# Giving out the final scatters of a graph-network kernel without a wait for their descriptors

## The chip, the cores and the metric

The kernel runs on one core of a Trainium2 chip. The metric is the device time of one execution in microseconds (us), lower is better. Engines: TensorE (PE in the profile, PEld for its weight loads), VectorE (DVE), ScalarE (ACT), GpSimd (POOL) and SyncE (SP), each with its own instruction stream and synchronised by semaphores alone.

## What is computed

`x` has 100,000 rows of 128 float32 values; there are 25,000 edges `src -> dst`, sorted by `dst`. Two graph layers follow each other, each with a residual and a layer norm. Cut to what matters:

```python
dst = minimum(int(100000 * uniform(25000) ** 2.0), 99999)     # then sorted

def _L0_gnn_ref(x, edge_index, W1, b1, W2, b2):
    row, col = (edge_index[0], edge_index[1])
    x_col = x[col]
    feat = jnp.concatenate([x_col, x[row] - x_col], axis=-1)
    messages = jax.nn.relu(feat @ W1 + b1) @ W2 + b2
    out = jax.ops.segment_max(messages, col, num_segments=x.shape[0])
    return jnp.where(jnp.isneginf(out), jnp.zeros_like(out), out)

def _L1_gnn_ref(x, edge_index, W1, b1, W2, b2, Wres, bres):
    agg = jax.ops.segment_sum(x[src], dst, num_segments=x.shape[0])
    h = jnp.maximum((x + agg) @ W1 + b1, 0.0) @ W2 + b2
    return x @ Wres + bres + h

x = _layernorm(x + _L0_gnn_ref(x, ...))
x = _layernorm(x + _L1_gnn_ref(x, ...))
```

Most rows are the `dst` of no edge. For them both sums are zero, and the result is a dense function of the row alone.

## The kernel before, in words

**Two kinds of work.** The dense work computes every one of the 100,000 rows as though it had no edge, and stores it to `out`. The edge work computes the rows that have edges and writes them over the dense result by scatters. `dst` is cut into groups of 512 edges (`ROWS`), 49 of them (`GROUPS`), each of four tiles of 128 (`TILES`): 196 tiles. The dense rows are cut into 196 units of 512 rows; four units are a body of 2,048 rows, and there are 49 bodies.

**Stages.** `walk` (line 310) lays out the same order on every engine: one dense body; the search for places of `src` among the edges (`step_s`); the edge pass of the first layer (`step_a`); that of the second (`step_b`); and dense bodies alone to the end. Dense units are woven into all of them. The second edge pass ends by writing its rows into the large SBUF buffer `edge_rows` (`finish1`, lines 1214 to 1222), which counts `res_done` up once per group.

**Dense units.** SP loads 512 rows into `x_in` (`load`, line 370), DVE normalises them (`norm1_scale`, line 712, whose multiplication is the helper's line 682), PE transposes and multiplies, ACT writes `o_rows` (line 1123) and SP stores them (line 385), counting `stored[k]` up by 16 per unit, k being the unit's place in its body.

**POOL.** Apart from some constants it only issues indirect DMAs: 196 gathers of `x` rows by `src`, 196 by `dst`, 196 of the table of first-layer results, and behind them the 196 scatters of `edge_rows` to `out`. All are issued one after the other in straight-line code. The scatter loop (lines 638 to 656) does this for each group:
- it waits until the scatters of four groups ago have landed (`final[r]`) and until the second edge pass has written the group (`res_done`);
- it waits until the dense stores have passed the group: the count comes from `stores_16`, in which DVE has put, from the group's last `dst`, 16 times the number of the body that holds it; `stores_needed` (line 634) loads it ahead of the last tile of the group before. The last, incomplete group (line 648) waits for all 49 bodies;
- it issues four scatters of 128 rows. Rows that are not the last edge of their `dst` have an index out of bounds and are dropped.

Line 656 waits for the landing of all scatters.

Of the kernel before, what the change touches and what calls it, by code (L numbers as in the profile page):

```python
# [44 lines left out]
def gnn_program(nc, x, src, dst, e_w1, e_b1, e_w2, e_b2, w1, b1, w2, b2, wres, bres, out):  # L45
    N, D = x.shape
# [20 lines left out]
    with ctx:  # L67
# [487 lines left out]
        def _(pool):  # L555
# [16 lines left out]
            def pace(kw):  # L572

                issued[0] += 1
                if issued[0] % 2 == 0:
                    kw["engine_sem"] = s_issued

            def issued_pair():
                if issued[0] % 2 == 0:
                    pool.wait_ge(s_issued, issued[0] // 2)  # L580
# [7 lines left out]
                issued_pair()  # L588

            def scatter(table, frm, t, done):  # L590
                kw = {}
                pace(kw)
                nc.gpsimd.indirect_dma_start(table, bass.IndirectOffsetOnAxis(idx[:, SCAT, t:t + 1], 0), frm, None,  # L593
                                             bounds_check=N - 1, oob_is_err=False, **kw).then_inc(done, 16)
                issued_pair()

            def gather_src(g):
                j, r = divmod(g, SLOTS)
# [41 lines left out]
            for g in range(GROUPS):  # L640
                j, r = divmod(g, SLOTS)
                wait(pool, final[r], 16 * TILES * j)
                pool.wait_ge(res_done, g + 1)
                if g < WHOLE:
                    for k in range(SLOTS):
                        pool.wait_ge(stored[k], count)
                    pool.nop().then_inc(s_turn, 1)
                elif g == WHOLE:
                    for k in range(SLOTS):
                        pool.wait_ge(stored[k], 16 * BODIES)  # L650
                for t in range(TILES):
                    if t == TILES - 1 and g + 1 < WHOLE:
                        count = stores_needed(g + 1)
                    scatter(out, edge_rows[:, cut(g * TILES + t)], g * TILES + t, final[r])
# [817 lines left out]
```

## Time and profile before

| | us |
|---|---|
| median of 3 runs | 1343.35 |
| lowest and highest run | 1338.25, 1344.81 |
| profiled execution | 1332.02 |
| its span, from first to last instruction | 1330.2 |
| mean granted TensorE clock | 0.952 |

| engine | busy us | share of the span |
|---|---|---|
| PE | 1123.7 | 84% |
| DVE | 1068.6 | 80% |
| POOL | 825.8 | 62% |
| ACT | 799.8 | 60% |

How to read it: the shares are means over all stages, and the stages have different limits, so the stretches and the end of the run have to be looked at one by one. POOL's busy time is the time in which it works at indirect DMAs, not the time in which data moves. "issue" as a releaser means that the profile shows nothing that the engine waited for. A line marked q (POOLq, SPq) is the engine's sequencer.

### The profile page before, as it was taken

To read this page: it belongs to the slowest core of one execution; us is meant where nothing else is said; L and a number is where in the kernel's file an instruction comes from. 1 tells how busy PE (TensorE), PEld (TensorE's weight loads), DVE (VectorE), ACT (ScalarE), POOL (GpSimd) and SP (SyncE) were. 2 spreads that over 40 slices of the span, in tenths; PEclk is the share of its full clock that TensorE was granted. 3 is DMA by queue.
4 is the path that set the end of the run, shared out by engine and by line. 5 is a ranking of instruction groups with operands and counts; after the bars stand their busy time and mean duration, and the time that the engine had idled before them with its cause. 6 is when DMAs were issued, how large, how long until landed. Compare 5 with 4: busy or idle time off the path is not lost. (4 is left out here: it accounts for less than half of the span.)

```text
span 1330.2 us, 32137 instructions
## 1 busy us (share of the span) xinstructions
PE 1123.7 (84%) x7512; PEld 853.2 (64%) x7512; DVE 1068.6 (80%) x5491; ACT 799.8 (60%) x2305; POOL 825.8 (62%) x797
## 2 busy tenths in 40 slices
PE   2699999998888878788759999999999999999500
PEld 1577777765555545455448888888887777777400
DVE  6599999989887887898838999999987888888400
ACT  0366666666665656667526666666666777777400
POOL 5666666656666666666256666666665666655654
PEclk9899999999998999999979999999999999999855
DMA  4477777756665667666436565656564556656310
GB/s 111 141 220 214 214 220 212 222 188 195 183 208 180 199 174 210 177 205 196 141 112 191 187 185 186 185 187 187 189 190 140 177 181 190 185 181 200 103 38 28
DMA packets 160366, 233.86 MB, mean 176 GB/s; under 512 B 26815, under 2 KB 69273, under 8 KB 160284
## 3 DMA queue, kind: packets, MB, share of 16 engines
q1 hardware_dynamic: 133612, 193.69, 46.7%
q0 software_dynamic: 25088, 38.81, 11.0%
q10 hardware_dynamic: 1584, 0.53, 0.2%
q14 instruction: 62, 0.51, 0.1%
q8 instruction: 20, 0.33, 0.1%
HBM read 129.48 MB, written 90.12 MB: 165 GB/s over the span
## 5 line engine op out<-in xcount | busy, mean ns | idle before, releaser
L1277 PE MATMUL psY<-wcr,xT 128*128 128x128 f32 x1568 | 305.0, 276 | 0.0
L1276 PE MATMUL psY<-wc,hT 128*128 128x128 f32 x1568 | 304.6, 276 | 0.0
L586 POOL DMA_INDIRECT edge_rows<-x1e_table,idx x196 | 210.8, 1075 | 133.2 <-DMA edge_rows<-x1e_table,idx 77.6
L593 POOL DMA_INDIRECT out<-edge_rows,idx x196 | 202.2, 1031 | 129.5 <-issue 76.4
L586 POOL DMA_INDIRECT edge_rows<-in_x,idx x196 | 206.9, 1056 | 116.0 <-DMA edge_rows<-in_x,idx 67.3
L586 POOL DMA_INDIRECT xd_rows<-in_x,idx x196 | 203.5, 1038 | 115.9 <-DMA xd_rows<-in_x,idx 67.3
L1276 PEld LDWEIGHTS psY<-wc,hT 128*128 128x128 f32 x1568 | 255.8, 193 | 15.0 <-issue 8.3
L1123 ACT ACTIVATE o_rows<-psY,rs_b 128x128 f32<-128x128 f32 x784 | 223.0, 367 | 66.7 <-DVE rs_b L741 66.5
L1277 PEld LDWEIGHTS psY<-wcr,xT 128*128 128x128 f32 x1568 | 239.9, 193 | 0.0
L1287 PE MATMUL psH<-xT,wc 128*128 128x512 f32 x392 | 204.5, 604 | 16.0 <-DVE deltas L787 10.6
L1103 ACT ACTIVATE sd_a<-mv_a,eps_col 128x4 f32<-128x4 f32 x196 | 58.3, 298 | 239.6 <-DVE mv_a L677 239.6
L672 DVE BATCH_NORM_STATS2 bn_b<-psY 128x6 f32<-128x128 f32 x784 | 174.4, 285 | 21.9 <-PE psY L1277 7.9
L691 DVE BATCH_NORM_STATS2 bn_a<-x_in 128x6 f32<-128x128 f32 x784 | 173.1, 271 | 0.3 <-DMA x_in<-in_x 0.3
L1267 PEld LDWEIGHTS psT<-ident,x 128*128 128x128 f32 x784 | 99.5, 143 | 106.2 <-issue 104.9
L1092 ACT ACTIVATE hT<-psH,bias_cols 128x512 f32<-128x512 f32 x196 | 131.0, 669 | 5.0 <-PE psH L1287 5.0
L682 DVE TENSOR_TENSOR x<-x_in,rs_a 128x512 f32<-128x512 f32 x196 | 130.6, 666 | 0.3 <-PE psT L1267 0.3
L1267 PE MATMUL psT<-ident,x 128*128 128x128 f32 x784 | 119.5, 276 | 0.9 <-DVE idx L1055 0.9
L1267 PE MATMUL psE<-ident,xs_rows 128*128 128x128 f32 x392 | 61.8, 281 | 60.8 <-ACT ehT L1161 51.6
L1100 ACT COPY xT<-psT 128x512 f32<-128x512 f32 x196 | 112.5, 574 | 0.5 <-PE psT L1267 0.5
L1267 PEld LDWEIGHTS psE<-ident,xs_rows 128*128 128x128 f32 x392 | 45.9, 143 | 98.2 <-issue 83.0
L923 DVE TENSOR_TENSOR_SCAN shared<-mask,shared,psE 128x512 f32<-128x512 bf16 x48 | 61.4, 1279 | 36.5 <-PE psE L1267 23.5
L1287 PEld LDWEIGHTS psH<-xT,wc 128*128 128x128 f32 x392 | 65.8, 194 | 35.6 <-issue 11.0
(135 smaller groups left out, 2042.6 us busy)
## 6 DMA issues: line engine op xcount, KB each, us to landing
x_in<-in_x SPq DMA_DIRECT2D x196, 256.0 KB
out<-o_rows SPq DMA_DIRECT2D x196, 256.0 KB
xs_rows<-edge_rows SPq DMA_DIRECT2D x98, 256.0 KB, 2.9
xs_rows<-src_dram SPq DMA_DIRECT2D x49, 256.0 KB, 4.3
mask<-mask_dram SPq DMA_DIRECT2D x98, 128.0 KB, 3.6
x1e_table<-shared SPq DMA_DIRECT2D x49, 256.0 KB, 2.8
x1eT_spill<-x1eT SPq DMA_DIRECT2D x49, 256.0 KB
x1eT<-x1eT_spill SPq DMA_DIRECT2D x49, 256.0 KB, 2.8
```

The source lines that it names most:

```text
L586: nc.gpsimd.indirect_dma_start(to, None, table, bass.IndirectOffsetOnAxis(idx[:, what, t:t + 1], 0), bounds_check=rows - 1, oob_is_err=err ...
L593: nc.gpsimd.indirect_dma_start(table, bass.IndirectOffsetOnAxis(idx[:, SCAT, t:t + 1], 0), frm, None, bounds_check=N - 1, oob_is_err=False ...
L672: last = v.bn_stats(bn[:, t, :], rows[:, cut(t)])
L682: v.tensor_tensor(tiles(to), tiles(rows), rs.unsqueeze(2).broadcast_to([P, TILES, P]), ALU.mult).then_inc(done, 1)
L691: last = v.bn_stats(bn_a[:, k % 2, t, :], x_in[:, k, cut(t)])
L1092: a.activation(hT[:, k % 2, :], psH[:, :], ACT.Relu, bias=bias_cols[:, 2:3]).then_inc(hT_done, 1)
L1100: a.copy(xT[:, k, :], psT[:, :]).then_inc(xT_done, 1)
L1123: last = a.activation(o_rows[:, k, cut(t)], psY[k % 2][:, cut(t)], ACT.Copy, scale=rs_b[:, k, t:t + 1])
L1267: last = t_.transpose(to[:, cut(t)], rows[:, cut(t)], ident[:, :])
L1276: t_.matmul(to[:, cut(t)], h[:, cut(t)], wc2[:, :], start=False, stop=False, skip_group_check=True)
L1277: last = t_.matmul(to[:, cut(t)], xt[:, cut(t)], wcr[:, :], start=False, stop=t == TILES - 1, skip_group_check=True)
L1287: t_.matmul(psH[:, :], wc1[:, :], xT[:, k, :], start=True, stop=True).then_inc(w1_done, 1)
```

## The change

The helper that issues the scatters no longer calls `pace` and `issued_pair`. The scatters carry no semaphore for their descriptors and no wait stands behind them. The gathers still count and wait by pairs; 588 of them come before the first scatter, an even number. The waits for landings, for `res_done` and for the dense stores are all kept.

```diff
             def scatter(table, frm, t, done):
-                kw = {}
-                pace(kw)
                 nc.gpsimd.indirect_dma_start(table, bass.IndirectOffsetOnAxis(idx[:, SCAT, t:t + 1], 0), frm, None,
-                                             bounds_check=N - 1, oob_is_err=False, **kw).then_inc(done, 16)
-                issued_pair()
+                                             bounds_check=N - 1, oob_is_err=False).then_inc(done, 16)
```

## Rows read from the trace of the kernel before

**Rows 1.** Busy time of each engine in four stretches of the end; DMA queues

```profile
core 0: us, PE busy (x) PEld busy (x) DVE busy (x) ACT busy (x) POOL busy (x), PEclk, DMA share, GB/s
...
1060.00:1130.00 70.00, 69.62 (x470) 54.71 (x469) 61.80 (x389) 54.40 (x164) 44.12 (x42) 1.00 0.61 187
1130.00:1200.00 70.00, 69.61 (x474) 54.94 (x473) 61.61 (x388) 54.92 (x164) 43.27 (x40) 1.00 0.61 183
1200.00:1256.00 56.00, 49.27 (x338) 39.35 (x336) 40.89 (x254) 40.53 (x123) 33.44 (x34) 0.98 0.52 164
1256.00:1331.00 75.00, 0.00 (x0) 0.00 (x0) 0.00 (x0) 0.00 (x0) 39.88 (x41) 0.50 0.11 33
...
q0 software_dynamic: 25088, 38.81, 11.0%
```

**Rows 2.** The end: last scatters, waits of SP and POOL, DRAIN (count: ns, starts)

```profile
1318.73 0.98 POOL L593 DMA_INDIRECT out<-edge_rows,idx  x1 [0.81 <-DMA out<-edge_rows,idx]
1320.02 0.98 POOL L593 DMA_INDIRECT out<-edge_rows,idx  x1 [0.30 <-issue]
...
L656 POOLq EVENT_SEMAPHORE  x2: 43/1508/2974, 1319.1 to 1319.2; - x2
...
L67 POOLq DRAIN  x1: 7589/7589/7589, 1322.4 to 1322.4; - x1
...
L550 SPq EVENT_SEMAPHORE  x2: 17/22/27, 1253.7 to 1255.0; - x2
```

**Rows 3.** POOL's timeline: first pair of scatters, and two groups behind the dense loop

```profile
991.37 1.02 POOL L593 DMA_INDIRECT out<-edge_rows,idx  x1 [2.00 <-issue]
992.69 1.00 POOL L593 DMA_INDIRECT out<-edge_rows,idx  x1 [0.30 <-issue]
...
1303.06 0.98 POOL L593 DMA_INDIRECT out<-edge_rows,idx  x1 [1.08 <-issue]
1304.35 0.98 POOL L593 DMA_INDIRECT out<-edge_rows,idx  x1 [0.30 <-issue]
1306.14 0.98 POOL L593 DMA_INDIRECT out<-edge_rows,idx  x1 [0.81 <-DMA out<-edge_rows,idx]
1307.43 0.98 POOL L593 DMA_INDIRECT out<-edge_rows,idx  x1 [0.30 <-issue]
1309.49 0.98 POOL L593 DMA_INDIRECT out<-edge_rows,idx  x1 [1.08 <-issue]
```

**Rows 4.** All 196 scatters: durations, first and last start, what POOL waited for

```profile
L593 POOL DMA_INDIRECT out<-edge_rows,idx x196: 975/982/1417, 991.4 to 1320.0; - x196
its engine sat idle before it (us, times) until:
  issue: 76.4, 134
  DMA out<-edge_rows,idx: 40.8, 50
  DMA out<-o_rows: 11.5, 10
```

**Rows 5.** Scatters as a group, from 1016 to 1200 us and from 1256 us on

```profile
L593 POOL DMA_INDIRECT out<-edge_rows,idx x107 | 114.1, 1066 | 70.9 <-issue 40.3 <-DMA out<-edge_rows,idx 21.3 <-DMA out<-o_rows 9.3
...
L593 POOL DMA_INDIRECT out<-edge_rows,idx x41 | 40.2, 981 | 25.4 <-issue 16.5 <-DMA out<-edge_rows,idx 9.0
```

**Rows 6.** POOL's sequencer: loading the count, and its last waits on stores

```profile
L635 POOLq TENSOR_LOAD <-stores x48: 284/290/809, 989.4 to 1305.9; - x48
L635 POOLq FUSED_REGOPS  x48: 147/147/181, 990.0 to 1306.2; - x48
...
L646 POOLq EVENT_SEMAPHORE  x2: 43/43/43, 1302.1 to 1308.5; - x2
```

**Rows 7.** SP's timeline around three dense stores (units 183, 191 and 195)

```profile
1216.62 0.42 SPq L385 DMA_DIRECT2D out<-o_rows  x1
...
1241.45 0.33 SPq L385 DMA_DIRECT2D out<-o_rows  x1
...
1252.94 0.33 SPq L385 DMA_DIRECT2D out<-o_rows  x1
```

**Rows 8.** Timeline where a scatter begins beside the multiplication of line 682

```profile
1067.80 0.69 DVE L682 TENSOR_TENSOR x<-x_in,rs_a 128x512 f32<-128x512 f32 x1
...
1067.94 1.40 POOL L593 DMA_INDIRECT out<-edge_rows,idx  x1 [0.81 <-DMA out<-edge_rows,idx]
```

**Rows 9.** All runs of line 682 from 1016 to 1200 us

```profile
L682 DVE TENSOR_TENSOR x<-x_in,rs_a x54: 655/658/692, 1016.3 to 1198.4; 128x512 f32<-128x512 f32 x54
```

## The prediction, made before the changed kernel was built or run

> **What bounds the kernel now.** I read the engines by stretch first, then the end of the run, then POOL's waits, then single scatters in order of time.
>
> By stretch [rows 1], PE is busy for 69.6 of 70 us up to 1200 us, so the dense loop sets the time there, with DVE second at 61.6 to 61.8. After 1256 us PE, DVE and ACT do nothing, and POOL alone works on: 41 scatters. This is the whole case: the dense loop stores its last rows and the span goes on for some 74 us in which only the scatters of line 593 are left.
>
> The end [rows 2]: the last stores have landed at 1255.0 us (SP's wait on line 550), the last scatter begins at 1320.02, POOL's wait for landings began at 1319.17 and took 2.97 us, and a DRAIN of 7.59 us follows. From the last scatter's start to the end of the span (1330.2) it is 10.2 us. The chain of waits names only that last scatter, so it doesn't tell why it was so late; the timeline does.
>
> The spacing [rows 3, 4]: 196 scatters start between 991.4 and 1320.0, one per (1320.0 - 991.4) / 195 = 1.685 us. In a quiet group, behind 1256 us, one takes 0.98 us. Between the two of a pair the engine is idle for 0.30 us; behind a pair it is idle 0.81 us inside a group and 1.08 us between groups, where POOL's sequencer also goes through the waits on the stores. So a pause costs 0.51 or 0.78 us over the bare spacing, and POOL's own waits [rows 4] tell the same: 76.4 us of "issue" and 40.8 us behind scatters, but only 11.5 us for the dense stores. POOL is hardly ever held by the data it scatters over; it is late because of its own rate.
>
> **What the change does, step by step.** It removes line 594's semaphore and line 595's wait. Nothing is added, no transfer is added or taken away, and the 588 gathers ahead of 991 us are as before, so I take the first scatter to start at 991.4 still.
>
> *The spacing without pauses.* Inside a pair it is 0.98 + 0.30 = 1.285 us (1303.06 to 1304.35, [rows 3]). No row shows a third scatter behind a second without a pause, so this has to be bounded. From below: 1.285, since the second of a pair had nothing to wait for and still came 0.30 us behind the first. From above: the present mean, 1.685. I go by the second of a pair, the nearest row, because only the number in the queue differs. Where the dense loop runs beside them the scatters are longer: the mean is 1.066 us from 1016 to 1200 us and 0.981 behind 1256 [rows 5], so I use 1.066 + 0.305 = 1.371 for the whole stretch with dense work.
>
> *Does the sequencer keep up?* Per group it has to load the count (0.29 us, with 0.15 us of register work) and go through the waits. But its wait of line 656 starts at 1319.1 us, before the last scatter starts on the engine at 1320.02 [rows 2], and the load at the fourth scatter of a group leaves the gap at 0.30 us as often as not [rows 3, 6]. It runs at least one instruction ahead, so I cost both at nothing; their cover is the 0.98 us of the scatter that is running. Were the cover gone, it would be the 0.27 us by which 1.08 exceeds 0.81, times 48 groups: 13 us.
>
> *POOL's clock.* The last group is the 49th: 192 scatters lie ahead of it. They take 192 x 1.371 = 263.2 us, so POOL comes to it at 1254.6 us; by the bare 1.285 it would be 1238.1.
>
> *The dense stores.* A group may go once all bodies up to the one that holds its last row are stored. By the way in which dst is drawn, the last row of group g lies near 100000 x (512 (g + 1) / 25000)^2. For g = 46 that is 92,700, body 45, whose last unit (183) is stored from 1216.62 us on; for g = 47 it is 96,600, body 47, unit 191, issued at 1241.45 us [rows 7]. I add the 2.1 us from 1252.94 to 1255.0 for landing: 1218.7 and 1243.6. POOL reaches these groups at 991.4 + 184 x 1.371 = 1243.7 and 991.4 + 188 x 1.371 = 1249.1, later than both. The 49th needs every store: 1255.0. That is what is late next. The two meet almost exactly (1254.6 against 1255.0), and any faster spacing gains nothing more.
>
> *The end.* From the last wait on the stores to the scatter behind it takes 1.0 us (1308.5 to 1309.49, [rows 6, 3]): first scatter of the last group at 1256.0, fourth at 1256.0 + 3 x 1.285 = 1259.9, end of span 10.2 us later at 1270.1. The span falls by 60.1 us.
>
> *What the faster scatters do to the dense loop.* The same bytes are moved in about four fifths of the time. The DMA engines are at 0.61 of their time there [rows 1] and all software transfers are 11% of the whole run's, so I expect some 0.03 more, and no cost. DVE: the scale of line 682 and the scatters meet. Where a scatter starts inside line 682's run it takes 1.40 us in place of 0.98 (start at 1067.94 beside a scale from 1067.80 to 1068.49, [rows 8]); where the scale starts inside a scatter it stays at 655 to 692 ns over all 54 of them [rows 9]. So the waiting is all on POOL's side, it is in the 1.066, and DVE loses nothing.
>
> The Trainium skill speaks against this (SBUF — State Buffer, Who interferes with whom): a VectorE instruction with two inputs in SBUF and a GpSimd instruction that reads SBUF exclude each other, and whichever was issued first holds the other up to its end. The trace agrees for the scatter that comes second and not for the scale that comes second: no scale of the 54 is longer than 0.692 us. By the rule in full a scale would often wait for a scatter, which is rival D.
>
> *Against the runs shown.* The profiled execution took 1332.02 us beside its span of 1330.2, and is 11 us below the median of 1343.35. I take the difference in time, 60 us, off the median: 1283 us, 4.5% faster.
>
> **Rivals.**
>
> A, the spacing is longer than a pair shows. For: the durations vary with what runs beside them, and a queue with more in it may be slower. Against: the second of a pair is no longer than the first. At 1.45 us the last scatter starts at 991.4 + 195 x 1.45 = 1274.2, and the time is 14 us above the forecast, 1297; at 1.5 us 1307. Chance 0.12, some of it above 1305.
>
> B, the pause isn't what sets the rate: without it a third scatter waits as long for something else, for instance for an earlier one to leave the queue. A scatter lands about 2.1 us after its start [rows 2], so with two allowed in the air the spacing would be near 1.1, which speaks against it, but no row excludes another limit near 1.6. Then nothing changes: 1343. Chance 0.09. That the change doesn't do what it says is in this too: the wait on s_issued would be gone and the spacing stay.
>
> C, slower: scatters given out without a pause get longer themselves. It decides where busy time and gap exceed 1.72 us ((1320.0 + 6.7 - 991.4) / 195), that is with a scatter above 1.41 us. The longest of all 196 is 1.417 [rows 4], next to line 682. Were all as long as that, and the gaps no shorter than today's mean of (0.30 + 0.81) / 2 = 0.56 us, (1.417 + 0.56) x 195 = 386 us would put the end at 1387, 57 us up: 1400. Against: the mean of 1.066 leaves room for one such scatter in five, (1.066 - 0.981) / (1.40 - 0.98). Chance 0.05.
>
> D, the scale waits for scatters (the rule above). A scatter would be at work for 0.98 / 1.285 = 76% of the time in place of 0.98 / 1.6 = 61%; half its length is 0.49 us, so each of the 75 units would wait 0.07 us longer: 5 us if all of it reached PE. DVE is idle for 8 of 70 us [rows 1], which hides it. Time 1283 to 1288. Chance 0.02.
>
> **How the numbers follow.** My forecast has 0.72: spacing at most 1.39, the stores decide, 1283, own range 1275 to 1292. A has 0.12, B 0.09, C 0.05, D 0.02. A measurement of this kernel can tell about 0.5% from no change. Faster by more than that: forecast, D and A, 0.86. Same: 0.09. Slower: 0.05. The range runs from 1273 (a run as much below the forecast as the shown ones spread) to 1305, the larger part of A; B, C and the rest of A are left out, under 0.2.
>
> **What would show it.** Right: scatters 1.29 to 1.4 us apart with gaps of 0.30 us throughout; the wait behind POOL's last group named as the dense stores, from about 1250 to 1256 us; last scatter near 1260; span near 1270; PE's 69.6 of 70 us unchanged; scales still under 0.7 us. Wrong: gaps above 0.30 between scatters that wait for no store (B), durations above 1.1 us behind the dense loop's end (C), PE under 69 of 70 us (the faster scatters cost the dense loop), or a last store later than 1255.

## The result, and the profile after

The changed kernel took 1488.02 us, the median of 4 runs (1468.92 to 1489.70), beside 1340.80 us before (4 runs, 1337.31 to 1344.81): a ratio of 1.106, 95% interval 1.097 to 1.116. It is 10.6% slower; 1283 us was forecast. The profiled execution took 1488.20 us, its span is 1486.3.

A call (a series of runs on one chip, one after the other) came in one of two kinds; the versions that lose much in one kind lose nothing in the other, and the profile of before, on which the prediction rests, is of the other kind than the timed runs of after. The experiments tell how that was found.

First the scatters, answering to [rows 3, 4]. All of them, with what POOL waited for:

```profile
L591 POOL DMA_INDIRECT out<-edge_rows,idx x196: 979/982/1208, 999.2 to 1476.3; - x196
its engine sat idle before it (us, times) until:
  DMA out<-o_rows: 183.8, 10
  issue: 103.4, 186
```

POOL's timeline after the change: the first three, and the last two groups (start us, length us, engine, line, operation; in brackets the idle time before it and what ended it).

```profile
999.19 1.21 POOL L591 DMA_INDIRECT out<-edge_rows,idx  x1 [2.00 <-issue]
1000.70 1.00 POOL L591 DMA_INDIRECT out<-edge_rows,idx  x1 [0.30 <-issue]
1002.00 0.98 POOL L591 DMA_INDIRECT out<-edge_rows,idx  x1 [0.30 <-issue]
...
1464.28 0.98 POOL L591 DMA_INDIRECT out<-edge_rows,idx  x1 [0.30 <-issue]
1472.40 0.98 POOL L591 DMA_INDIRECT out<-edge_rows,idx  x1 [7.14 <-DMA out<-o_rows]
...
1476.26 0.98 POOL L591 DMA_INDIRECT out<-edge_rows,idx  x1 [0.30 <-issue]
```

The change did what it says. The gap is 0.30 us where POOL's own sequencer isn't held up with the others ("issue" is 0.56 us in the mean over 186 scatters, since some of it lies in the standstill told below), the wait for POOL's own completion is gone, no scatter is longer than before (1.208 us against 1.417 at most), and the waits behind which POOL stands are now those for the dense stores: 183.8 us in place of 11.5. POOL is no longer late by its own rate. It is the dense loop that is late, by stretch, to be held against [rows 1]:

```profile
core 0: us, PE busy (x) PEld busy (x) DVE busy (x) ACT busy (x) POOL busy (x), PEclk, DMA share, GB/s
1060.00:1130.00 70.00, 27.70 (x79) 18.46 (x79) 10.90 (x55) 7.43 (x21) 48.19 (x50) 0.54 0.22 69
1130.00:1200.00 70.00, 17.06 (x66) 11.68 (x65) 9.65 (x51) 8.60 (x27) 49.66 (x51) 0.56 0.19 60
1200.00:1256.00 56.00, 42.42 (x249) 32.91 (x250) 33.23 (x209) 30.07 (x89) 16.69 (x17) 0.82 0.37 115
1256.00:1331.00 75.00, 70.35 (x468) 54.77 (x468) 61.28 (x385) 54.53 (x165) 11.78 (x12) 1.00 0.48 151
```

In 70 us PE begins 79 matmuls where it began 470, the DMA engines move 69 GB/s in place of 187, and no engine but POOL is busy for more than 40% of the time. Everything but the scatters nearly stands still. The granted clock of 0.54 is a mean close to the lower level, 1.2 GHz. It fell between 1011 and 1012 us, and PE, still granted 1.00, had begun nothing from 1009 us on: the fall follows from the standstill. Nor do the transfers that are under way take longer: from 1060 to 1200 us the queue of the loads and stores moves 1,963 packets in 7.4% of the 16 DMA engines' time, 84 ns each, in place of 11,732 in 51.6%, 99 ns each. Fewer are given out. At 1221 us POOL has given out what it may (it waits for stores from there on), and the dense loop is back at its old speed. Seven dense stores are issued from 1012 to 1218 us, where it had been one every 3.4 to 11 us.

What it looks like inside shows in PE's timeline; these are matmuls of one accumulation (first of psY, then of psE), between which the code has no wait:

```profile
1060.98 0.37 PE L1273 MATMUL psY<-wc,hT 128*128 128x128 f32 x1 [0.83 <-issue]
1061.70 0.37 PE L1273 MATMUL psY<-wc,hT 128*128 128x128 f32 x1 [0.35 <-issue]
1062.42 0.57 PE L1274 MATMUL psY<-wcr,xT 128*128 128x128 f32 x1 [0.35 <-issue]
...
1084.60 0.37 PE L1273 MATMUL psE<-wc,ehT 128*128 128x128 f32 x1 [1.72 <-issue]
1087.41 0.37 PE L1274 MATMUL psE<-wcr,x1eT 128*128 128x128 f32 x1 [2.44 <-issue]
1089.51 0.37 PE L1274 MATMUL psE<-wcr,x1eT 128*128 128x128 f32 x1 [1.72 <-issue]
```

They start 0.72, 0.72, then 2.81 and 2.10 us apart: steps of about 0.70 us. "Issue" means that the profile shows nothing they waited for. I call a stretch of over 0.70 us in which none of PE, DVE, ACT and SP starts anything a silence. From the first scatter to the end of PE's work the trace of after has 83 of them, 127 us in all, most about 0.70 or 1.40 us long, the first at 1007 and the last at 1214 us. The trace of before has none. The silences are the plainest sign of the harm and not the whole of it: the last dense store, shown next, comes 216 us late.

The end answers to [rows 2, 7]. The last dense store, on SP:

```profile
1469.22 0.33 SPq L385 DMA_DIRECT2D out<-o_rows  x1
...
L67 POOLq DRAIN  x1: 7589/7589/7589, 1478.5 to 1478.5; - x1
```

It was 1252.94 us in the trace of before, which is of the other kind, so it is 216.3 us later. The prediction's working for the end, put behind this store, gives 1469.22 + 2.1 + 1.0 = 1472.3 for the last group (measured 1472.40), 1476.2 for the last scatter (1476.26) and 1486.4 for the span (1486.3). All that is wrong with the forecast is the time of the dense loop: 1270.1 + 216.3 = 1486.4.

### The profile page after: what moved, and what is told of

Read it like the earlier page. It is cut to its first block, busy times and chain, and to the rows that moved or that the text cites. A ratio compares the mean times of both kernels' runs of the same rounds, so it can differ in the third digit from the quotient of the medians.

```text
span 1486.3 us, 32134 instructions
## 1 busy us (share of the span) xinstructions
PE 1177.7 (79%) x7512; PEld 877.3 (59%) x7512; DVE 1071.3 (72%) x5491; ACT 802.0 (54%) x2305; POOL 809.5 (54%) x797
## 4 chain that ended last, share of the span: by engine, by line
PE 40%; DVE 22%; issue 15%; another core or an unknown queue 10%; ACT 7%; DMA 3%; SPq 1%; POOL 1%; DVEq 1%; ACTq 0%; POOLq 0%
PE psY L1274 7%; PE psY L1273 7%; PE psH L1284 6%; DVE bn_b L669 4%; PE psE L1264 4%; PE psT L1264 3%; DVE bn_a L688 3%; PE psY L1270 2%; PE psE L1274 2%; PE psE L1273 2%; DVE shared L873 2%; DVE x L679 2%; PE psE L1423 2%; ACT xT L1097 2%
## 5 line engine op out<-in xcount | busy, mean ns | idle before, releaser
L591 POOL DMA_INDIRECT out<-edge_rows,idx x196 | 192.8, 984 | 287.2 <-DMA out<-o_rows 183.8
L1273 PE MATMUL psY<-wc,hT 128*128 128x128 f32 x1568 | 310.1, 279 | 8.8 <-issue 8.8
L1274 PE MATMUL psY<-wcr,xT 128*128 128x128 f32 x1568 | 310.2, 279 | 6.9 <-issue 6.9
L586 POOL DMA_INDIRECT edge_rows<-x1e_table,idx x196 | 204.2, 1042 | 136.5 <-issue 99.9
L1273 PEld LDWEIGHTS psY<-wc,hT 128*128 128x128 f32 x1568 | 260.4, 196 | 26.2 <-issue 19.3
L1284 PE MATMUL psH<-xT,wc 128*128 128x512 f32 x392 | 211.2, 621 | 50.1 <-ACT xT L1097 38.9
L1274 PEld LDWEIGHTS psY<-wcr,xT 128*128 128x128 f32 x1568 | 244.0, 196 | 10.4 <-issue 10.4
L1264 PE MATMUL psT<-ident,x 128*128 128x128 f32 x784 | 122.7, 279 | 4.0 <-issue 3.1
L669 DVE BATCH_NORM_STATS2 bn_y<-psE 128x6 f32<-128x128 f32 x196 | 43.4, 284 | 97.6 <-remote 75.8
```

What stands on the lines that cost most here:

```text
L586: nc.gpsimd.indirect_dma_start(to, None, table, bass.IndirectOffsetOnAxis(idx[:, what, t:t + 1], 0), bounds_check=rows - 1, oob_is_err=err ...
L669: last = v.bn_stats(bn[:, t, :], rows[:, cut(t)])
L1264: last = t_.transpose(to[:, cut(t)], rows[:, cut(t)], ident[:, :])
L1273: t_.matmul(to[:, cut(t)], h[:, cut(t)], wc2[:, :], start=False, stop=False, skip_group_check=True)
L1274: last = t_.matmul(to[:, cut(t)], xt[:, cut(t)], wcr[:, :], start=False, stop=t == TILES - 1, skip_group_check=True)
L1284: t_.matmul(psH[:, :], wc1[:, :], xT[:, k, :], start=True, stop=True).then_inc(w1_done, 1)
```

## The experiments

Eighteen runs of fifteen kernels in six calls, each call on one chip. Where no interval is given a time is a single run. They are told in the order in which they ran, since what the first ten seemed to show fell with the later ones.

### Call 1 (chip 2; before 1346.87 us): how many scatters are handed over ahead, and how many go without a pause

Two kernels let POOL issue without a gap but only while at most 2 or 4 scatters are unfinished (`DEPTH`); two others put the old wait back behind every fourth or eighth scatter (`EVERY`).

```diff
+                if given[0] >= DEPTH:
+                    pool.wait_ge(s_given, given[0] - DEPTH + 1)
+                given[0] += 1
                 nc.gpsimd.indirect_dma_start(table, ...,
+                                             engine_sem=s_given).then_inc(done, 16)
```

```diff
+                given[0] += 1
+                if given[0] % EVERY == 0:
+                    kw["engine_sem"] = s_given
                 nc.gpsimd.indirect_dma_start(table, ..., **kw).then_inc(done, 16)
+                if given[0] % EVERY == 0:
+                    pool.wait_ge(s_given, given[0] // EVERY)
```

At most two unfinished. Expected:

> No pause, but the sequencer hands over a scatter only when at most one other is unfinished: one at work, one waiting. Spacing as in the changed kernel (gaps of 0.30 us). Theory Q (the queue of handed-over scatters, 5 to 7 deep when PE stopped in the changed kernel, is what starves the other engines): the dense loop keeps its pace, PE 69 of 70 us, last scatter near 1260, time 1275 to 1295. Theory W (what starves them is that POOL's engine works with gaps of only 0.30 us, whatever waits behind it): the dense loop stops as in the changed kernel, time above 1440.

At most four unfinished. Expected:

> The same with at most four unfinished. Theory Q: if the limit lies above four, the time of the run with two, 1275 to 1295; if it lies below, some stops, 1300 to 1488. Theory W: above 1440, the same as with two.

A pause behind every fourth. Expected:

> A wait behind every fourth scatter in place of every second. Mean spacing (0.98 x 4 + 0.30 x 3 + 1.08) / 4 = 1.48 us where no scale is in the way. Theory Q: at most three wait, so it should be as the run with four unfinished: last scatter near 1285, time 1295 to 1315. Theory W: gaps of 1.08 us every 6 us give the others some relief; between 1300 and 1440.

A pause behind every eighth. Expected:

> A wait behind every eighth scatter. Theory Q: up to seven can wait, as many as when PE stopped: clearly slower than before, above 1380, and PE's instructions missing in the last third of each eight. Theory W: above 1400.

Measured: 1471.76, 1487.93, 1388.03 and 1469.08 us. With at most two unfinished the loss is nearly whole (71 silences, scatters 1.287 us apart as in the changed kernel), where theory Q gave 1275 to 1295: the number that waits in POOL's queue is not the cause. A pause behind every fourth takes most of the lost time away (1388.03, in the range of theory W), but only about half of the dense loop's delay: its last store comes at 1368.9 us, 116 us behind the trace of before, and PE is busy for 50.57 and 56.30 of 70 us in the stretches from 1060 and from 1130 us, with 7 silences in all. So the loop also slows down without silences.

### Call 2 (chip 14; before 1333.46 us, 1332.20 to 1337.14, 7 runs): something else in the pause's place, threes, gathers, and a free tail

The first writes 128x512 int32 of zeros to a spare buffer behind every second scatter, with no wait; the second keeps the scatters in pairs and gives the gathers a wait behind every fourth; the third waits behind every third scatter (`EVERY = 3` above); the fourth keeps pairs up to scatter 160 and lets the last 36 run free.

```diff
+                if t % 2 == 1:
+                    wait(pool, s_fill, filled[0] - 3)
+                    nc.gpsimd.memset(filler[:, filled[0] % 4, :], 0).then_inc(s_fill, 1)
+                    filled[0] += 1
```

```diff
-                if issued[0] % 2 == 0:
-                    pool.wait_ge(s_issued, issued[0] // 2)
+                if issued[0] % 4 == 0:
+                    pool.wait_ge(s_issued, issued[0] // 4)
```

```diff
+                if t < FREE_FROM:
+                    pace(kw)
```

A write in place of the pause. Expected:

> No wait, but behind every second scatter POOL writes zeros over 128x512 int32 of a scratch buffer (one such took 0.52 us in the kernel before), so the scatters keep about the spacing of the pairs while POOL's engine gets no rest and its sequencer runs ahead by up to some seven scatters. Theory D (it is the scatters' own work, the writing of their descriptors, without a break of about 0.8 us in it): the dense loop keeps its pace, PE above 69 of 70 us, time near 1343. Theory W (any work of POOL's engine without rest): slow, above 1440. Theory Q (the queue), which the runs with two and four handed over speak against: slow as well.

Gathers by four, scatters in pairs. Expected:

> The kernel before with its 588 gathers waited for behind every fourth in place of every second; scatters in pairs. If what starves the engines comes with indirect DMAs of any kind (D or W), the stages before 990 us get longer, as the run with scatters by four did, by 5 to 40%: time above 1370, and the first scatter starts later than 1000 us. If it comes with scatters alone (their writes to HBM), the gathers end earlier or as before: time 1325 to 1345.

A pause behind every third. Expected:

> A wait behind every third scatter. Theories D and W: a burst of three lies between pairs (no loss) and fours (1388): the time is the sum of POOL's gain, 196 x 0.07 = 14 us, and what the dense loop loses; 1320 to 1365. If the loss sets in only at the fourth, 1330; if every burst of three costs as much as those of four, above 1370.

A free tail. Expected:

> The kernel before with pairs up to the 160th scatter and no wait from there on. In the trace of the kernel before the 160th comes at about 1259 us, when the dense loop has ended, so nothing is left to starve. Theories D, W and Q alike: 36 scatters at 1.285 in place of some 1.66 us: last scatter 13 us earlier, time 11 to 14 us less, near 1330. If the change itself costs something for another reason (a longer end), there is no gain.

Measured: 1302.78, 1320.64, 1311.36, and for the free tail 1324.27 us (1322.30 to 1324.82, 4 runs; ratio 0.992, interval 0.990 to 0.994). No silence in any. The write makes a gap of 0.72 us and a mean spacing of 1.53 us, and does no harm. Three of the four came out below every range that was given: the write was expected near the old spacing and 1343 us, the threes at 1320 or more, the gathers by four at 1325 or more; the free tail gained 9 us, where 11 to 14 were expected. So here it seemed that any rest for POOL will do, and that threes are harmless where fours are not. That comparison went across two calls, and it was a mistake.

### Call 3 (chip 5; before 1342.94 us): where the rest stands and how long it is

The same write in other sizes and places: two of 128x512 behind every fourth scatter, one of 128x256 behind each, one of 128x16 behind each; and the gathers without any wait, with the scatters in pairs.

```diff
+                if t % EVERY == EVERY - 1:
+                    for _ in range(REPS):
+                        wait(pool, s_fill, filled[0] - 7)
+                        nc.gpsimd.memset(filler[:, filled[0] % 8, :], 0).then_inc(s_fill, 1)
+                        filled[0] += 1
```

```diff
             def gather(to, table, what, t, done):
-                kw = {}
-                pace(kw)
...
-                issued_pair()
```

Fours with a rest. Expected:

> No wait; behind every fourth scatter two writes of 128x512 int32 (0.55 us each). Bare spacing (3 x 1.285 + 0.98 + 1.10 + 0.17) / 4 = 1.53 us on average, a little slower than the 1.49 of the run with one write behind every second, which cost the dense loop nothing. Theory B (what counts is how many scatters come in a row: three do no harm, four do): slow like the run with a wait behind every fourth, 1350 to 1400. Theory R (what counts is the mean rate: something takes up a scatter in about 1.5 us, and a backlog forms below that): as good as that run, 1300 to 1312.

A write behind each. Expected:

> No wait; behind every single scatter one write of 128x256 int32 (0.31 us): bare spacing 0.98 + 0.31 + 0.17 = 1.46 us, never two scatters in a row. Theory B: the dense loop untouched, last scatter near 1280, time 1285 to 1298. Theory R with a limit between 1.48 and 1.53: slow, 1350 to 1430.

A small write behind each. Expected:

> The same with a write of 128x16 int32, about 0.11 us: bare spacing about 1.26 us, no slower than the changed kernel's 1.285. Theory B, if any other instruction breaks the row: dense loop untouched, the stores decide, 1275 to 1285. Theory B, if it takes a break of some length, and theory R: 1440 to 1490.

Gathers without waits. Expected:

> The kernel before with no wait behind any of its 588 gathers; scatters in pairs. If the harm comes with any indirect DMA in long rows, the stages before 990 us get much longer: above 1450. If it comes with scatters alone, POOL's gathers end earlier: 1290 to 1325.

Measured: 1382.48 (5 silences), 1433.70 (17), 1487.07 (97) and 1774.31 us. Fours with writes stand where fours with waits stood (1388.03): it isn't the wait itself that heals. A rest behind each scatter, so that the short gap of 0.30 us is gone altogether, does worse (4 us above the range of theory R) than rests behind every fourth with gaps of 0.30 within: the short gap isn't what does the harm. Its mean spacing is shorter (1.48 against 1.53 us), which speaks for the rate; but these are single runs 3% apart in spacing, and where nothing else holds them up the fours with a wait come to 1.48 us as well (as expected above) and the write behind each to 1.473. That the rate decides is the simplest reading, not shown; that a long rest helps more than several short ones would fit too.

The write of 128x16 lies inside the gap of 0.30 us that is there anyway, so the rate is the changed kernel's, and so is the loss, in time the same within the spread of the changed kernel's own runs. Gathers given out without waits harm too, from the start of the run. Busy tenths of the page, in 40 slices of 44 us:

```profile
PE   3110149999877777777762111117999999999995
PEld 1110137777645444454442000006888888777774
DVE  4000049999777676776761000007988988888883
```

Slices 2 to 5 and 22 to 27 are the standstill; all of it lies before the first scatter, at 1179 us, or within a slice of it. So it isn't a matter of scattering, nor of the direction of the transfers (one run).

### Call 4 (chip 3; before 1336.35 us): threes, pairs with a short gap, and half the bytes

Threes with the 128x512 write; pairs with the 128x256 write (mean spacing 1.416 us); and the changed kernel with 64 of the 128 rows of each tile.

```diff
-                nc.gpsimd.indirect_dma_start(table, bass.IndirectOffsetOnAxis(idx[:, SCAT, t:t + 1], 0), frm, None,
+                nc.gpsimd.indirect_dma_start(table, bass.IndirectOffsetOnAxis(idx[0:P // 2, SCAT, t:t + 1], 0),
+                                             frm[0:P // 2, :], None,
```

The last leaves half of the scattered rows out. Expected:

> No wait; behind every third scatter one write of 128x512 int32, so a gap of 0.72 us and a mean bare spacing of (2 x 1.285 + 0.98 + 0.72) / 3 = 1.42 us. Theory B (rows of at most three with a gap of 0.7 us or more between them do no harm): dense loop untouched, last scatter near 1272, time 1275 to 1290. Theory R (mean rate): below the 1.46 us that already did harm, so 1400 to 1488.

> No wait; behind every second scatter one write of 128x256 int32: pairs with a gap of 0.50 us between them, mean bare spacing 1.38 us. Theory B, if the length of the row alone counts: untouched, 1275 to 1290. Theory B, if a gap below 0.7 us doesn't end a row (as the run with 0.50 us behind every single one suggests), and theory R: slow, 1420 to 1488.

> The changed kernel with only the first 64 of each 128 rows scattered: half of the scattered rows are left out, so its output differs and its time is to be read for the pace of the dense loop alone. If it is the number of scatters a microsecond, or the share of time in which POOL works on them: as slow as the changed kernel or slower for as long as the row of scatters lasts. If it is the number of rows (descriptors) a microsecond: harmless if a scatter of 64 rows still takes 0.9 us or more (dense loop untouched, near 1272); harmful if it takes about half the time.

Measured: 1296.98, 1278.03 and 1273.84 us, no silence in any. The pairs with a short gap, by stretch:

```profile
1060.00:1130.00 70.00, 69.62 (x467) 54.30 (x467) 61.69 (x386) 54.89 (x164) 58.53 (x75) 1.00 0.62 193
1130.00:1200.00 70.00, 69.60 (x472) 54.93 (x472) 61.84 (x392) 54.60 (x163) 58.27 (x76) 1.00 0.60 196
1200.00:1256.00 56.00, 49.86 (x343) 39.94 (x341) 41.28 (x257) 41.19 (x125) 46.77 (x60) 0.97 0.50 170
```

POOL issues 75 scatters in 70 us in place of 42 (the count holds the writes too, half as many: 50 scatters), and PE is busy for the same 69.62 us. This fits the first case of theory B, 1275 to 1290; the threes with a write lie 7 us above that theory's range and 100 below the other's. The half rows are harmless with scatters of 0.90 us, as the theory of rows had it, but the whole rows of the short gap are harmless beside them, so they say nothing for it. In call 3 a longer spacing, 1.48 us, had cost 91 us. A rule by spacing can't hold both, and all harmed kernels had come from three calls, all unharmed ones from two. The traces then showed a second thing that goes by the call, in a part of the run where every kernel but two has the same code: the first stage.

### Calls 5 and 6: the same kernels again

Nothing is edited: the changed kernel and the pairs with a short gap in one call (chip 14, which had been unharmed in call 2), and the changed kernel once more in the last (chip 1). Expected:

> The changed kernel itself once more, nothing edited. All harmed runs so far came from three calls and all harmless ones from two others, each call on one chip, and the harmed traces hold about half as many semaphore records (13,177 to 15,577) as the others (29,665 to 30,108) already in the gather stage, where the code is the same. Theory 1 (the rate or the spacing of the scatters alone does the harm, wherever it runs): 1465 to 1490 us, whatever the number of records, and about 80 to 100 silences of all engines. Theory 2 (the harm needs a chip of one kind, on which the records are halved): on a chip of the halved kind 1465 to 1490; on one that records about 30,000 there are no silences, and the time is about 1270 to 1285, as the prediction had it and as the kernel of half rows ran (1273.84). So a run at 1465 or more with about 30,000 records speaks for theory 1, a run below 1300 for theory 2, and 1465 or more with 14,000 records leaves it to the kernel of pairs beside it.

> The kernel with a 128x256 write behind every second scatter (spacing 1.41 us in the mean), which ran 1278.03 us with no silence where about 30,000 records were kept. Theory 1 (the rate or spacing alone): 1275 to 1285 here too, on any chip, 4 to 5% faster than before. Theory 2 (the chip decides, and with it any spacing below some 1.5 us does harm): on a chip of the halved records 1400 to 1460, as the write behind each scatter had it at 1.473 us (1433.7); on a chip with about 30,000 records 1275 to 1285.

> The changed kernel once more, nothing edited, in a call of its own. The kernel of the short gap ran 1278.03 us in one call and 1477.73 in another, on chip 14, which had earlier run four kernels unharmed: so neither the kernel nor the chip alone decides, but something that holds for a whole call and shows itself in the trace as about 14,000 semaphore records in place of about 30,000 and, with the same code, in a first stage that is about 10 us longer (gather 197 at 340 to 343 us in place of 331 to 332). Theory 1 (state of the call): where this call has about 30,000 records and gather 197 at 331 to 332, the changed kernel has no silence in its last stage and runs 1268 to 1285 us, with before at 1332 to 1337; where it has about 14,000, 1465 to 1510, with before at 1337 to 1347. Theory 2 (scatters spaced by 1.285 us stop the engines in any call): 1465 to 1510 with about 30,000 records too.

Measured. Call 5, with before at 1339.47 us (1337.00 to 1345.77, 7 runs): the changed kernel 1489.30 us (1477.09 to 1506.66, 4 runs; ratio 1.110, 1.099 to 1.120), the pairs with a short gap **1477.73 us** (1475.65 to 1495.67, 5 runs; ratio 1.102, 1.098 to 1.106), where they had taken **1278.03**. Call 6, with before at 1338.72 us (7 runs): the changed kernel 1485.37 us (1472.85 to 1495.17, 4 runs; ratio 1.106, 1.100 to 1.111). The same stretches of the same kernel as above, in call 5:

```profile
1060.00:1130.00 70.00, 27.51 (x127) 19.96 (x127) 16.97 (x86) 13.98 (x42) 56.07 (x74) 0.67 0.29 89
1130.00:1200.00 70.00, 24.66 (x89) 17.11 (x88) 12.84 (x64) 9.27 (x28) 55.99 (x74) 0.55 0.23 72
1200.00:1256.00 56.00, 43.84 (x264) 34.63 (x265) 34.84 (x212) 31.21 (x93) 15.70 (x22) 0.84 0.35 114
```

This is shown, then: one program, 200 us apart, by the call in which it runs (one run in call 4, five in call 5). 1477.73 lies outside both ranges that were given for it. The changed kernel never met the other kind, so its two runs here fit either theory. Chip 14 had both kinds, going by the marks below, so the chip alone doesn't decide. And the first stage tells the kinds apart before any scatter: the stretch from 150 to 250 us of the pairs with a short gap in call 4, and below it in call 5.

```profile
150.00:250.00 100.00, 99.94 (x871) 78.12 (x870) 98.54 (x512) 61.82 (x178) 64.47 (x62) 1.00 0.71 215
```

```profile
150.00:250.00 100.00, 96.65 (x805) 71.38 (x805) 92.50 (x478) 57.72 (x165) 64.41 (x63) 1.00 0.67 202
```

PE, busy all the time in the one, loses 3.3% in the other and DVE 6%, at the same clock, while POOL gives out one gather per 1.6 us in both. The table has what I read for every run. Spacing is the mean of the first hundred between scatters; records are all semaphore updates that the trace holds; gaps are those of over 0.5 us between two such records from 100 to 300 us, in the stage that nearly all share; gather 197 is its start. The time is the median of the kernel's runs and is set beside that of before in the same call; under "loop" stands the issue of the last dense store. All but the time is read from the profiled execution, which took 1495.67 us for the short gap in call 5 and 1479.92 and 1495.17 us for the changed kernel in calls 5 and 6.

| run | call | spacing us | records | gaps | gather 197 | silences | loop us | time us | against before |
|---|---|---|---|---|---|---|---|---|---|
| before (profiled execution) | – | 1.697 | 29,921 | 14 | 331.4 | 0 | 1252.9 | 1332.02 | |
| gathers by four | 2 | 1.701 | 29,665 | 10 | 326.3 | 0 | 1247.8 | 1320.64 | -13 |
| free tail | 2 | 1.698 | 29,969 | 15 | 332.6 | 0 | 1256.5 | 1324.27 | -9 |
| threes | 2 | 1.577 | 30,025 | 10 | 332.1 | 0 | 1254.4 | 1311.36 | -22 |
| pairs, write | 2 | 1.528 | 30,001 | 11 | 332.3 | 0 | 1253.8 | 1302.78 | -31 |
| threes, write | 4 | 1.487 | 29,896 | 17 | 331.5 | 0 | 1256.0 | 1296.98 | -39 |
| pairs, short gap | 4 | 1.416 | 30,108 | 10 | 332.1 | 0 | 1253.5 | 1278.03 | -58 |
| free, half rows | 4 | 1.252 | 29,889 | 9 | 331.7 | 0 | 1256.1 | 1273.84 | -63 |
| fours, wait | 1 | 1.527 | 13,660 | 149 | 341.4 | 7 | 1368.9 | 1388.03 | +41 |
| fours, writes | 3 | 1.528 | 13,177 | 150 | 340.0 | 5 | 1363.4 | 1382.48 | +40 |
| write behind each | 3 | 1.481 | 14,366 | 143 | 341.0 | 17 | 1414.1 | 1433.70 | +91 |
| pairs, short gap | 5 | 1.427 | 14,108 | 161 | 343.5 | 91 | 1476.4 | 1477.73 | +138 |
| two unfinished | 1 | 1.454 | 13,887 | 147 | 341.4 | 71 | 1452.6 | 1471.76 | +125 |
| eights | 1 | 1.437 | 14,137 | 152 | 341.8 | 66 | 1450.0 | 1469.08 | +122 |
| changed kernel | – | 1.407 | 14,175 | 150 | 342.3 | 83 | 1469.2 | 1488.02 | +147 |
| changed, 2nd | 5 | 1.436 | 13,977 | 155 | 340.4 | 67 | 1460.9 | 1489.30 | +150 |
| changed, 3rd | 6 | 1.422 | 14,145 | 151 | 340.6 | 95 | 1476.2 | 1485.37 | +147 |

Of those left out, four unfinished and the small write stand beside the changed kernel (14,223 and 13,986 records), and the gathers without waits (15,577) slow the first stage themselves. Three things can be read off it.

- Two kinds of call, and nothing between. In one the trace has about 30,000 semaphore records, in the other about 14,000 of the same program's. In the second they come in bursts some 0.78 us apart, already in the first stage: 139 to 161 gaps in 200 us against 9 to 17. The number of instruction records is the same in both (32,134 for each of the three runs of the changed kernel, 32,137 before).
- In the second kind the loss is larger where the spacing is shorter: 40 us at 1.53, 91 at 1.48, 122 to 150 below (in the last dense store 110 to 116, 161, and 197 to 224 us behind 1252.9). Below, the measured spacing has the standstill in it (without it it is 1.29 for the changed kernel), and the changed kernel alone spreads from 1468.92 to 1506.66 us, so there is no order among these. Before itself, at 1.70 or so, loses 2 to 13 us, going by its times in the calls of either kind: 1338.72 to 1346.87 against 1333.46 and 1336.35. Its single runs overlap (1336.09 in call 6, 1337.14 in call 2), so its time doesn't tell the kind.
- In the first kind nothing is lost down to 1.416 us with whole scatters and 1.252 with half rows, and the time follows POOL's last scatter.

## Why the prediction was wrong

*The spacing without pauses*: right. It was bounded by 1.285 and 1.685 and taken as 1.371; alone, the scatter comes 1.285 us behind the last [rows 3, and the timeline above], with no third or tenth scatter later than the second. Rival B (0.09) is refuted by all three runs of the changed kernel. Whether 1.371 was right beside the dense loop is open, since the changed kernel never ran beside an undisturbed one. By the mean length from 1016 to 1200 us, the 0.086 us of lengthening was 0.09 for threes with a write (1.069 us), 0.03 for pairs with a short gap (1.008) and 0.04 for the half rows (0.947 against 0.90).

*Does the sequencer keep up?* Right. In the half rows, where nothing stood still, the idle time put down to "issue" is 54.1 us over 172 scatters, 0.31 us each, the fourth of a group included, and in the changed kernel up to seven further scatters have been handed over when the engine begins one.

*The dense stores* and *the end*: right. Put behind the last store as it was, the forecast's steps give the start of the last group to 0.1 us in both kinds of call. In the half rows the last store is issued at 1256.13 us and the steps give 1259.2:

```profile
1247.65 0.90 POOL L591 DMA_INDIRECT out<-edge_rows,idx  x1 [18.04 <-DMA out<-o_rows]
...
1259.30 0.91 POOL L591 DMA_INDIRECT out<-edge_rows,idx  x1 [7.12 <-DMA out<-o_rows]
...
1262.92 0.90 POOL L591 DMA_INDIRECT out<-edge_rows,idx  x1 [0.30 <-issue]
```

The wait of 7.12 us in front of the last group is the forecast's "what is late next": the stores, no longer POOL. The span ends 9.1 us behind this kernel's last scatter, not 10.2. With a mean spacing of 1.416 the last scatter should start at 990.6 + 195 x 1.416 = 1266.7, and the span end 10.2 us later at 1276.9; the pairs with a short gap have 1266.0 and 1276.2 in call 4. That is the pricing of rival A.

*What the faster scatters do to the dense loop*: this is the step that failed. I expected some 0.03 more of the DMA engines' time and no cost. In the trace of after the last dense store is 216.3 us later, more than three times the gain of the rest. The bytes were not the reason (the DMA engines' share fell from 0.61 to 0.22 and 0.19), the scaling of line 682 neither: it is line 679 in the changed kernel, runs there only 4 times from 1016 to 1200 us, and its longest is 687 ns, against 692 [rows 9]. The rule of the Trainium skill (SBUF — State Buffer, Who interferes with whom), from which rival D was made, would hold a scale for a scatter that was issued first. [rows 9] were weaker evidence against it than I took them for: of the 54 scales only 6 begin inside a scatter. The trace still disagrees with a scatter every 1.416 us beside an undisturbed loop, where 50 of the 54 do and none is longer than 0.704 us (pairs with a short gap, call 4):

```profile
L689 DVE TENSOR_TENSOR x<-x_in,rs_a x54: 655/657/704, 1016.8 to 1199.0; 128x512 f32<-128x512 f32 x54
```

Rival C, the slower case (0.05), had the wrong mechanism: scatters did not get longer, they stayed at 982 ns. None of my cases held that scatters of the same length nearly stop all the other engines, and I had looked only at what the scatter shares with each engine in turn (a port, the DMA engines' time). The right row was missing as well: [rows 1] show scatters no denser than 42 in 70 us, one per 1.67 us, and in the harmed kind of call a large loss begins somewhere between that and 1.53. I bounded the spacing from both sides but not its cost to the loop, although no row of before shows what a denser stream does to it; that cost had no upper end, and the range should have shown it.

*Against the runs shown*: the second failure. The profiled execution was 11 us quicker than the median of the runs, and I carried that over as an offset. It was the sign of the other kind of call. Before takes 1333.46 and 1336.35 us in the calls of the first kind and 1338.72 to 1346.87 in the others, and the trace of before, by its 29,921 records and its gather 197 at 331.4 us, is of the first kind, the one in which a denser stream is harmless.

What stays open. *The changed kernel itself* ran in three calls, counting that of the result, and all three are of the harmed kind. That it would take about 1272 us in the other rests on its two nearest neighbours there, 1278.03 and 1273.84 us; it isn't measured. *What the kind of call is* isn't known. Neither the chip alone nor the kernel alone sets it. The bursts in the semaphore records, some 0.78 us apart, and the silences in steps of 0.70 us make one think of a path that is served every 0.7 to 0.8 us, which semaphore updates and the scatters' and gathers' work share, and which the recording of the execution may load as well. This is a guess, not shown. Every timed run here is a recorded one, so it is also open whether an execution that isn't recorded would lose anything. *Whether the rate decides*, and why, isn't shown either, and no spacing between 1.53 and 1.70 us was tried in the second kind.

## What to carry to other kernels

A short wait on POOL behind each pair of indirect DMAs looks like waste, and in one kind of call it is (4% here); in the other all the other engines nearly stop without it, for scatters (five calls, counting that of the result) and for gathers (one run). Where an engine's rate of issuing rises above any that the trace shows, the cost to everything beside it is unknown and has to be bounded as such, not summed from ports and bytes. Run a version in several calls before believing it, compare only within a call, and check a property of the trace that the change can't touch, such as the first stage's pace; when a profiled execution lies 1% off the median of the runs, find out why first. None of the versions tried here may replace before: those that gain 1 to 4% in one kind of call were not run in the other, or lost 10% there. Time a recorded and an unrecorded execution side by side where that can be had; here it is the largest open question.

## What the runs showed of the hardware that I had not expected

- Scatters given out 1.285 us apart, each 0.98 us long, left PE busy for 17 to 28 of 70 us, DVE for 10 to 11 and ACT for 7 to 9, with matmuls 0.70, 1.40 or 2.1 us apart, in a call whose semaphore records come in bursts. Pairs with a short gap (mean spacing 1.42 us) left PE at 25 to 28 of 70 us in such a call and at 69.6 in another.
- The loss in such a call does not go by the shortest gap: writes behind each scatter, with gaps of about 0.49 us between scatters and a mean spacing of 1.48 us, lose 91 us; fours with gaps of 0.30 and a mean of 1.53 lose 40.
- Once POOL has to wait for stores and gives out four scatters at a time, the loop runs at nearly its old pace in the same call: PE 70.35 of 75 us from 1256 to 1331.
- A write of 128x16 int32 behind a scatter costs nothing (spacing 1.288 against 1.287 in the changed kernel): it lies in the gap of 0.30 us; 128x256 makes the spacing 1.473. Half the rows shorten the scatter only from 0.98 to 0.90 us.
- Gathers waited for by fours in place of pairs brought the first scatter from 992.4 to 978.9 us within call 2 (write in place of the pause beside it) and the time from 1333.46 to 1320.64 us; one run, in the unharmed kind only.
